# A Flamingo block on one Trainium2 core: a later norm product, row-by-row waits in the first down half, the first attention behind the routed rows, and context squares on ScalarE

## The reference, cut to what matters

```
...
sim = stack([cos(emb, emb_left), cos(emb, emb), cos(emb, emb_right)])   # over the 128 rows, for each column
out = einsum('bit,oi->bot', unfold3(layernorm(x)) * repeat(sim, C), w_xattn)
x1  = x + tanh(g_xattn) * out
...
n      = layernorm(x1)
rw     = sum(top_2(n @ gate_w))
h      = relu(n @ up_w) ** 2
shared = h @ down_w
routed = ((n @ fc1_w) @ expert_w * rw) @ fc2_w
out    = x1 + tanh(g_ffn) * (layernorm(shared + routed) * gamma + beta)
```

## Time and profile before

| what | value |
|---|---|
| median of 3 executions | 993.27 us (991.49 to 993.35) |
| the profiled execution: its own time, its span | 992.8 us, 990.8 us |
| TensorE busy | 945.3 us, 95% of the span |
| VectorE, ScalarE, GpSimd busy | 491.2, 323.3 and 319.0 us |
| share of TensorE in the chain that ended last | 85% |
| first block: start of tile 4, of the first down half, of its third sample's rows | 94.22, 198.74 and 260.98 us |

### The profile page before, as it was taken

One profiled execution on the slowest core, in us unless ns is written; L12 is line 12 of the kernel. 1 busy time (PEld: TensorE's weight loads), 2 busy tenths in 40 slices (PEclk: granted clock), 3 DMA queues, 4 the chain that ended last, 5 costly groups with the idle time before them and its releaser, 6 DMA issues.

```text
span 990.8 us, 12369 instructions
## 1 busy us (share of the span) xinstructions
PE 945.3 (95%) x4562; PEld 441.1 (45%) x4562; DVE 491.2 (50%) x859; ACT 323.3 (33%) x437; POOL 319.0 (32%) x147
## 2 busy tenths in 40 slices
PE   4989599799999999999999999999999999999995
PEld 2448244344444444444444444444444444444442
DVE  6677678985762345365662236355563222211112
ACT  3578775743331123242321122233332122211111
POOL 4220322238572431242572422142672200001110
PEclk9999799889999999999999999999999999999998
DMA  8796976343414543323414443422324233200001
GB/s 318 258 350 234 358 277 216 87 128 86 125 46 128 177 150 131 109 86 86 127 43 129 163 144 130 130 86 85 100 71 128 86 107 107 64 1 21 9 14 43
DMA packets 63359, 127.15 MB, mean 128 GB/s; under 512 B 35250, under 2 KB 35378, under 8 KB 62146
## 3 DMA queue, kind: packets, MB, share of 16 engines
q1 hardware_dynamic: 62290, 124.04, 38.2%
q10 hardware_dynamic: 1008, 2.30, 0.8%
HBM read 100.96 MB, written 19.07 MB: 121 GB/s over the span
## 4 chain that ended last, share of the span: by engine, by line
PE 85%; DVE 4%; ACT 3%; DMA 2%; issue 2%; DVEq 1%; ACTq 1%; SPq 1%; POOL 0%
PE psS L1411 32%; PE psS L1357 20%; PE psR L1357 20%; PE psR L1421 8%; PE psP L1320 5%; DMA big<-in_w_fc 1%; DVEq L906 1%; DMA xT<-in_ctx 1%; ACT hid L801 1%; DVE s L935 0%; ACT hid L812 0%; DVE ring L971 0%; DMA sim_scratch<-simo 0%; ACTq L811 0%; DVE s L939 0%
## 5 line engine op out<-in xcount | busy, mean ns | idle before, releaser
L1411 PE MATMUL psS<-big,hid 128*128 128x512 f16 x1536 | 337.4, 381 | 6.9 <-issue 6.6
L1411 PEld LDWEIGHTS psS<-big,hid 128*128 128x128 f16 x1536 | 150.4, 98 | 189.2 <-issue 9.4
L1357 PE MATMUL psS<-xT,ring 128*128 128x512 f16 (+1 forms) x912 | 191.5, 370 | 3.8 <-DVE xT L1060 2.7
L1357 PE MATMUL psR<-xT,ring 128*128 128x512 f16 (+1 forms) x912 | 190.2, 368 | 0.0
L1357 PEld LDWEIGHTS psS<-xT,ring 128*128 128x128 f16 x912 | 89.9, 99 | 102.5 <-DVE xT L1060 2.8
L1357 PEld LDWEIGHTS psR<-xT,ring 128*128 128x128 f16 x912 | 89.3, 98 | 97.1
L542 POOL TENSOR_TENSOR y<-y,lgb 128x1024 f32<-128x1024 f32 x15 | 39.2, 2612 | 252.8 <-ACT y L679 252.8
L1078 DVE SCALAR_TENSOR_TENSOR y<-psR,rw,y 128x1024 f32<-128x1024 f32 x15 | 19.2, 1281 | 141.0 <-PE psR L1421 141.0
L1421 PE MATMUL psR<-w,lgb 128*128 128x512 f16 x384 | 85.5, 379 | 0.0
L512 POOL TENSOR_TENSOR sides<-scr 128x1024 f32<-128x1024 f32 x12 | 30.1, 2506 | 141.7 <-DMA scr<-in_ctx 141.7
L532 POOL TENSOR_TENSOR ring<-f_buf,ring 128x1024 f32<-128x1024 f32 x18 | 39.2, 2177 | 99.7 <-ACT f_buf L647 60.4
(11 more groups left out here) (203 smaller groups left out, 989.1 us busy)
## 6 DMA issues: line engine op xcount, KB each, us to landing
ring<-pair_scratch SPq DMA_DIRECT2D x60, 512.0 KB, 3.3
ring<-sim_scratch SPq DMA_DIRECT2D x18, 504.0 KB
big<-in_w_up SPq DMA_DIRECT2D x8, 1024.0 KB, 6.4
out_rows<-y SPq DMA_DIRECT2D x15, 512.0 KB, 3.0
hid<-in_w_down SPq DMA_DIRECT2D x14, 512.0 KB, 6.1
big<-in_w_down SPq DMA_DIRECT2D x14, 512.0 KB, 6.9
pair_scratch<-ring SPq DMA_DIRECT2D x12, 512.0 KB, 6.9
scr<-in_ctx SPq DMA_DIRECT2D x9, 576.0 KB, 3.8
```

Of the source, the lines that this page charges most:

```text
L1357: mm = pe.matmul(up_bank[t % NR][:, cols], rows[:, a, k, :], xT[:, k, b, cols], start=(k == 0 and a == 0 and b == 0), stop=(k == KB - 1 an ...
L1411: mm = pe.matmul(psS[:, HALF * h:HALF * h + HALF], hT[:, i, a, P * j:P * j + P], dn[:, i, b, HALF * h:HALF * h + HALF], start=(i == 0 and ...
```

## The change

- The `w2` norm product goes behind tile 6 on TensorE instead of tile 4, and `w2_scale` goes to tile 7 on VectorE (`W2_SCALE_T` from 5 to 7).
- The squares of the second block's contexts move from GpSimd to ScalarE, behind the relu of tiles 4, 7, 9 and 12. ScalarE waits there for GpSimd's shifted product (`prod1`).
- In the first down half sample 0 runs all 16 shared rows, then the routed rows, then the attention. Each shared row has its own two waits: its hidden row (`h_rdy`) and its down row (`dn_rdy`).
- The last three down rows are split ahead of the high and low parts of the attention's inputs, on ScalarE and on VectorE; the routing arithmetic comes behind them.
- `take_s`, `take_r`, `y_stats` and ScalarE's part of `finish` of sample 0 move ahead of sample 0's `combine` and its normalisation.
- Near the start, the second sample's transposed halves are evacuated ahead of one `w2` copy and one weight square on ScalarE, and ahead of a `combine` on VectorE.

```diff
-        W2_SUM_T, W2_SCALE_T = 3, 5
+        W2_SUM_T, W2_SCALE_T = 3, 7
...
-        XATTN_AT, XATTN_FIRST = (5, 0, 0, 0), (12, 12, 10, 6)
+        XATTN_AT, XATTN_FIRST = (5, 0, 0, 0), (None, 12, 10, 6)
...
                 pool.tensor_tensor(sides_a[:, :], scr_a[:, 0:T], scr_a[:, P:CTX], ALU.mult)
                 pool.drain().then_inc(prod1, 1)
+                if first:
+
+                    return
                 pool.tensor_tensor(scr_a[:, :], scr_a[:, :], scr_a[:, :], ALU.mult).then_inc(prod0, 1)
...
+                    if first and t in SIM_FIRST:
+                        act.wait_ge(prod1, BB + SIM_FIRST.index(t) + 1)
+                        act.activation(scr_a[:, :], scr_a[:, :], ACT.Square).then_inc(prod0, 1)
                     if first and EARLY + t < IT:
...
+                    for c in DN_LATE:
+                        dn_split_hi(c)
                 if phase_a:
                     f_his(m, 0)
...
                     if first and j == 0:
-                        for c in DN_LATE:
-                            dn_split_hi(c)
+
+                        act.wait_ge(f_lo_v, 2)
+                        act.wait_ge(f_lo_p, 1)
+                        take_s(n, j, phase_a)
                     if phase_a:
                         if j < BB - 1:
                             std(LX, BB * m + j + 1)
                             f_rows(m, j + 1)
+                        if first and j == 0:
+                            finish(n, j)
                         std(L1, BB * m + j)
                         x1_normal(m, j)
                         x_hi(m, j)
-                        if first and j == 0:
-                            take_s(n, j, phase_a)
...
             up_square(0)
-            up_square(1)
-            w2_evac(3)
             first_xt_hi(1, 0)
             first_xt_hi(1, 1)
+            w2_evac(3)
+            up_square(1)
...
+                if first:
+                    for c in DN_LATE:
+                        dn_lo(c)
+                    f_los(m, 0)
                 routing(n)
-                if phase_a:
+                if phase_a and not first:
                     f_los(m, 0)
...
                         if j < BB - 1:
                             x_stats(m, j + 1)
+                        if first and j == 0:
+                            take_r(n, j)
+                            y_stats(n, j)
                         combine(m, j)
                         x_lo(m, j)
...
             fc1_los(2, LT)
-            combine(0, 2)
             first_xt_lo(1, 0)
             first_xt_lo(1, 1)
+            combine(0, 2)
...
                     if first:
+                        pe.wait_ge(h_rdy, i + 1)
                         pe.wait_ge(dn_rdy, i + 1)
...
+                    if first and j == 0:
+
+                        pe.wait_ge(up_evac, UT - 2)
+                        shared(0, 0, IT, True).then_inc(s_done, 1)
+                        pe.wait_ge(up_evac, UT)
+                        pe.wait_ge(w2_rdy, LT)
+                        routed(0, 0, LT).then_inc(r_done, 1)
+                        xattn(m, 0)
+                        continue
                     if j == 0:
                         pe.wait_ge(up_evac, UT * (n + 1) - 2)
                         pe.wait_ge(h_rdy, IT * (n + 1) - 2)
-                        if first:
-                            pe.wait_ge(w2_rdy, LT)
...
```

More of the change, by code:

```diff
@@ L1214, in down_half @@
                         continue
-                    take_r(n, j)
-                    y_stats(n, j)
+                    if not (first and j == 0):
+                        take_r(n, j)
+                        y_stats(n, j)
             def last_rows():
```

17 lines of the change are left out of this document (7 added, 10 removed).

## The result

The changed kernel takes **999.57 us** (median of 4 executions, 998.57 to 1001.27) against 992.7 us of the kernel before (median of the three executions above and a fourth of 992.13): a ratio of 1.0076, 95% interval 1.006 to 1.0092. So it is slower by 0.8%, where the prediction had 993.8 us, a range up to 998.0, and "the same" as the likeliest outcome. The profiled execution took 999.63 us, its span is 997.6 us.

The account below looks back on a forecast made before the run. Two chains, TensorE's own work and GpSimd's, were taken to end together at the third sample's rows, with TensorE's shortened far more. Against 992.8 us, -4.6 + 3.1 + 0.4 + 2.1 = +1.0 gave 993.8 us, range 989.5 to 998.0.

Parts of the forecast that it names:

- the GpSimd chain: From `f_lo` of sample 1 to the third sample's rows: 31.65 us as before, plus 0.4 (bounds 0 and 1.2).
- `f_lo`: First down half: `f_lo` of sample 1 comes 3.1 us later against the up half's end (bounds 1.3 and 4.0).
- the clock: Third sample's rows: TensorE resumes after idling at the 1.2 GHz level, costing 2.1 us (bounds 0 and 2.4).
- the up half: Up half ends 4.6 us earlier: 5.8 plus 1.3 gained, 2.5 lost (bounds 1.1 and 7.4).
- from there GpSimd's work is unchanged: From `f_lo` of sample 1: same GpSimd operations through the store and `take_s`, with 0.4 us added for VectorE's low half.
- The norm product: Up half, tiles 4 to 12: ScalarE's waits for TensorE, together 5.8 us, are gained.
- The squares: Up half: four squares on ScalarE cost 2.5 us; without GpSimd's square VectorE gains 1.3 (bounds 0 and 2.6).
- ScalarE carries the squares: Rival in the up half: all four squares lie on ScalarE's path, gain 1.1 instead of 4.6, 997.3 us; chance 0.24.
- room of 2 to 3 us: First down half: attention ends at 216.7 us, VectorE needs it at 219.4.
- A rival had the clock fall inside the up half: TensorE idles between tiles, runs tiles 18, 19 and first rows slowly, the attention comes late: 996.2 us; chance 0.08.
- behind this there is no other new wait: Behind the third sample's rows: the next `take_s` follows the same chain with more room; nothing added.
- TensorE bounds: Rival in the down half: GpSimd's chain keeps up, rows of samples 0 and 1 run without stop, 978.3 us; chance 0.05.

Follow-up runs that it names:

- e6: The changed kernel with one wait added: VectorE's two low parts of sample 2 wait until GpSimd has finished sample 0; 995.2 us, 1.0038 of the kernel before.
- e11: The changed kernel with the `w2` norm product put back behind tile 4; 1000.63 us, 1.0088 of the kernel before.
- e9: The changed kernel with the squares of the second block's contexts put back on GpSimd; 1002.15 us, 1.0101 of the kernel before.
- e12: The changed kernel again, without any edit, on the same chip as the runs with one part undone; 997.56 us, 1.0058 of the kernel before.
- e5: The changed kernel with `take_r`, `y_stats` and ScalarE's part of `finish` of sample 0 behind the low parts of sample 1; 995.91 us, 1.0046 of the kernel before.
- e10: The changed kernel with the order near the start put back; 997.77 us, 1.0052 of the kernel before.
- e13: The changed kernel without 13 of TensorE's 16 per-row waits for hidden rows; 995.88 us, 1.0038 of the kernel before.
- e14: The kernel before with a separate wait for its hidden row at each of the 16 shared rows; 994.35 us, 1.0024 of the kernel before.
- e8: The changed kernel with GpSimd's `finish` ahead and ScalarE's `take_s` of samples 1 and 2 ahead of the next high parts; 984.15 us, 0.9926 of the kernel before.
- e15: The edits of e8 and e13 together on the changed kernel; 981.08 us, 0.9887 of the kernel before.
- e1: The changed kernel with gamma, beta and the first home addition ahead of `f_lo` of sample 1, three additions behind `finish`; 1002.96 us, 1.0104 of the kernel before.
- e2: The same edit as e1, made to the kernel before; 1004.01 us, 1.0116 of the kernel before.
- e3: The kernel before with only the up half's part: later norm product, context squares on ScalarE, order near the start; 987.85 us, 0.9953 of the kernel before.

## Why the prediction was wrong, step by step

**The mechanism was the right one.** The forecast said that the idle time moves to a wait of 10 us or more ahead of the third sample's rows, released by `take_s`, with GpSimd busy without a gap ahead of it and half clock behind it. That is what the trace shows. Its numbers for the places hold too: the norm wait is gone, the first down split comes 4.1 us earlier (3.5 to 6), `f_lo` of sample 1 stands at 229.65 (226 to 231). The rows start at 189.3 instead of 187. The time was wrong by 5.8 us. Of these the GpSimd chain has 2.0, the loop's way back 1.6, the start 1.4, the stage ahead of the last low half 0.8, `f_lo` 0.5 and the clock 0.4, less 0.9 from the up half:

**The GpSimd chain, +2.4 instead of +0.4 (bounds 0 and 1.2).** This is the step that failed: "from there GpSimd's work is unchanged", with one VectorE operation beside it. Three fell there. In the kernel before, the attention of sample 1 came late enough that VectorE made its low parts while GpSimd was past `finish`. TensorE now runs sample 1 earlier, and `x_lo` and both low parts of sample 2 land on `weigh` and `finish`. These three GpSimd operations are 2.6 us longer; 0.3 comes back, because `take_s` had stood directly behind ScalarE's high parts before (259.83, no idle time), so that GpSimd's chain had that much room. The operations to count were all those that the faster engine brings forward into the chain, not the nearest one. e6 shows 1.8 us of the term, those on `finish`; the 0.8 on `weigh` is read from the rows. The Trainium skill, SBUF — State Buffer, section "SBUF: two separate sides", has the rule that a VectorE operation with two SBUF inputs and a GpSimd operation take turns for whole instructions. The trace agrees that each loses beside the other: the GpSimd operations concerned are 0.8 to 1.0 us longer, and VectorE's low part takes 3.24 us, that of sample 1 in the same trace 1.21.

**The up half, -5.5 instead of -4.6, by two errors that nearly cancel.** The norm product was given 5.8 us and is worth 2.9 (e11): ScalarE's waits for TensorE were counted in full. With the later product alone (e9) they are gone, but between 95 and 165 us ScalarE then waits for VectorE's square of the relu 6.3 us instead of 5.0, and 2.4 instead of 0.8 without a named releaser: half of the 5.8 came back in other waits. The squares were given a net cost of 1.2 us and gain 2.6 (e9). The prediction took half of one 2.6 us difference for GpSimd's part, and said that its squares "cost nothing before on this path". By the timelines of e9 and e12 they delay VectorE by 1.0 us in the tile of the second square, and by 1.65 more where a low half, being that late, meets a product. So the rival "ScalarE carries the squares", which was to carry most of the chance of slower, had the sign of this term wrong.

**`f_lo`, +3.6 instead of +3.1.** Inside its bounds (1.3 to 4.0). e5 splits it: about 2.5 us `take_r` and `y_stats`, the rest, by the waits, the attention's later place. The prediction's room of 2 to 3 us between the attention and VectorE is what limits the first to 2.5.

**The clock, +2.5 instead of +2.1,** just over its bound of 2.4. A rival had the clock fall inside the up half as well. It did: tiles 18 and 19 took 12.21 us behind a wait of 3.26 us, 1.7 us more than at full clock, and the rows started at 189.3 instead of 187. It cost nothing, since VectorE came to `combine` at 221.06, after the attention; in e10, where these tiles ran at full clock, the third sample's rows start at 261.29, in e12 at 261.77. The Trainium skill, TensorE: Matmul & The Clock Gate, section "HAM oscillation — how this bites in real kernels", has bursts that restart at half clock after each wait. Here most do and one does not. TensorE in e10, at a granted clock of 1.00:

```profile
174.15 10.52 PE L1372 MATMUL psR<-xT,u_buf 128*128 128x512 f16 x48 [3.27 <-DVEq L1174]
```

**Not in the sum.** 0.8 us in tile 17 of this one execution, where a pair of VectorE's down rows beside GpSimd's `weigh` took 6.21 us (4.22 in e12). 1.6 us at the loop's way back (e13, e14): "behind this there is no other new wait" is where the prediction missed it, since it looked no further than the next `take_s`. 1.4 us at the start, likewise of this one execution.

**The rival that was set aside.** "TensorE bounds" had 978.3 us and a chance of 0.05. Its condition, that GpSimd's chain keeps up, was rightly denied; with that chain and `take_s` reordered (e8, and e15 with the shorter wait at the loop) the kernel takes 984.15 and 981.08 us.

## What to carry to other kernels

When a change lets one engine run ahead, list every operation on the other engines that comes forward with it, and look whether it now falls beside the operations of the chain that becomes the bound; count VectorE operations with two inputs in SBUF beside GpSimd's as a likely loss for both. A wait that only shows slack says where to look next, not what to move: the reordering that paid here (13.4 us from e12 to e8) put `finish` into a time when GpSimd waited for a load, and `take_s` ahead of other work, while moving additions ahead of a `keep` that others wait for made the changed kernel 3 to 5 us slower (e1) and the kernel before 12 us (e2). And a term that comes out right as a sum should be tested by its parts, since here an overrated 5.8 and a wrong sign made a 4.6 that came out near the measured 5.5.

## What the runs showed of the hardware

- A loop's way back costs TensorE 0.9 to 1.1 us or 2.2 to 2.7 us, switched by 13 wait instructions fewer (e13) or 16 more (e14) ahead of the loop. After the longer one the next 46 matmuls took 10.09 us in some executions (granted clock 1.00 in e12) and 11.78 in others (0.86 on the mean of 12 us in e8 and e9, so in part at the 1.2 GHz level); after the shorter one the clock was 1.00 (before, e2, e3, e13, e15). The Trainium skill, Runtime: NRT & Kernel Launch, section "Instruction fetch mechanics", says that a taken branch to instructions that are not at hand stalls until they are loaded. The trace agrees with a stall, and gives its size; what TensorE waits for there the profile does not name.
- A wait of 3.2 to 3.3 us ahead of tiles 18 and 19 was followed by half clock in most profiles (11.87 to 12.21 us for 48 matmuls) and by full clock in one (10.52, e10).
- VectorE operations that met ScalarE's squares of 128x1152 in e12 kept their usual time (0.68 to 0.69 and 1.22 us); beside GpSimd's square of the same size in e9 operations of 1.28 and 0.69 us took 2.65 and 2.59, and beside GpSimd's product one of 0.68 took 2.84.
